# One of eight scalings of the scan's inputs made by GpSimd instead of ScalarE

## What is computed

```python
x = einsum('bld,ed->bel', ctx, in_proj_w)            # (4, 512, 512)
u = silu(causal_conv4(x) + conv_b)
dt_low, Bm, Cm = split(einsum('bdl,ed->bel', u, x_proj_w), [16, 32], axis=1)
dt = softplus(einsum('brl,dr->bdl', dt_low, dt_proj_w) + dt_proj_b)
A = -exp(A_log)                                      # (512, 16)
def step(state, inp):                                # over the 512 positions
    d, b, c, u = inp
    state = state * exp(d[..., None] * A) + (d * u)[..., None] * b[:, None, :]
    return state, einsum('bdn,bn->bd', state, c)
y = (ys + D * u) * silu(layernorm(x0))
```

## Time and profile before

| | us |
|---|---|
| median of 3 runs | 1756.34 |
| lowest, highest | 1755.08, 1762.23 |
| the profiled execution | 1761.8 |
| its span, from the first to the last instruction | 1759.7 |
| scan loop in the profile: first scan, last product | 59.5 to 505.9 |
| mean granted TensorE clock over the span | 0.927 of full |

### The profile page before, as it was taken

How to read it: one execution, slowest core, us unless ns; L and a number is a source line. 1 busy time by engine, 2 the same in 40 slices (tenths; PEclk the granted TensorE clock), 3 DMA queues, 4 the chain that set the end, 5 groups by cost and what they waited for, 6 DMA issues and landing times. The chain is left out here.

```text
span 1759.7 us, 22630 instructions
## 1 busy us (share of the span) xinstructions
PE 1540.0 (88%) x6580; PEld 669.6 (38%) x6581; DVE 1177.1 (67%) x1726; ACT 1006.3 (57%) x1551; POOL 518.1 (29%) x314
## 2 busy tenths in 40 slices
PE   5688878879857999999998789589999999898997
PEld 1334334334432444444443333123333333244543
DVE  7688988989885222222225749568888888369875
ACT  3798988979933001111113332357777777678775
POOL 1478678678860710000005446340000000000000
PEclk7698988979978999999999889689999999999999
DMA  5101102002472545458526453543332333020000
GB/s 176 42 31 46 51 19 67 18 13 72 137 255 94 191 62 190 150 177 274 177 85 200 130 126 112 199 79 79 74 84 71 83 74 81 29 96 1 31 30 36
DMA packets 105352, 173.47 MB, mean 99 GB/s; under 512 B 18323, under 2 KB 52499, under 8 KB 104259
## 3 DMA queue, kind: packets, MB, share of 16 engines
q1 hardware_dynamic: 83750, 124.62, 24.4%
q0 software_dynamic: 6624, 23.14, 4.4%
q10 hardware_dynamic: 14912, 24.89, 4.2%
HBM read 109.29 MB, written 54.92 MB: 93 GB/s over the span
## 5 line engine op out<-in xcount | busy, mean ns | idle before, releaser
L1582 DVE TENSOR_REDUCE a_mx<-a_s 128x2 f32<-128x1024 f32 x256 | 301.1, 1218 | 58.5 <-PE a_s L1704 57.0
L255 POOL TENSOR_TENSOR m_hs<-m_hs,m_C 128x1024 f32<-128x1024 f32 x128 | 301.3, 2367 | 117.0 <-DVE m_hs L447 116.4
L447 DVE TENSOR_TENSOR_SCAN m_hs<-m_dA,m_d 128x512 f32<-128x512 f32 x256 | 296.9, 1205 | 53.6 <-PE m_d L584 32.9
L859 ACT ACTIVATE e_sg<-e_gu 128x256 f32<-128x256 f32 x63 | 24.2, 383 | 312.8 <-PE e_gu L1091 312.8
L584 PE MATMUL m_d<-ident_sb,m_dBuT 128*128 128x128 f32 x1024 | 169.4, 300 | 27.4 <-ACT m_dBuT L332 14.4
L584 PEld LDWEIGHTS m_d<-ident_sb,m_dBuT 128*128 128x128 f32 x1024 | 122.4, 151 | 176.3 <-DVE m_hs L447 104.9
L1724 PE MATMUL a_t<-ring_sb 99*128 99x512 bf16 x512 | 181.1, 393 | 7.2 <-ACT early_sb L1486 3.8
L1486 ACT ACTIVATE a_pr<-a_t 128x512 f32<-128x512 f32 x256 | 142.3, 596 | 63.1 <-PE a_t L1724 61.9
L353 ACT ACTIVATE m_dA<-m_dt,m_negA 128x512 f32<-128x512 f32 x256 | 170.4, 712 | 7.7 <-DVE m_hs L447 7.6
L1704 PE MATMUL a_s<-ring_sb 96*128 96x512 bf16 x512 | 152.8, 390 | 24.3 <-DMA ring_sb<-qk_dram 14.1
L1486 ACT ACTIVATE early_sb<-a_t 128x512 f32<-128x512 f32 x256 | 142.2, 596 | 51.6 <-PE a_t L1724 50.6
(11 more groups left out here) (308 smaller groups left out, 2386.3 us busy)
## 6 DMA issues: line engine op xcount, KB each, us to landing
ring_sb<-qk_dram SPq DMA_DIRECT2D x384, 64.0 KB, 2.8
e_w<-in_ex_gu SPq DMA_DIRECT2D x16, 1024.0 KB, 6.7
xg_dram<-zeros_sb SPq DMA_DIRECT2D x2, 6016.0 KB, 28.5
e_xg<-xg_dram ACTq DMA_DIRECT2D x47, 256.0 KB, 2.7
yg_dram<-e_yo ACTq DMA_DIRECT2D x47, 256.0 KB, 2.0
m_C<-c_dram SPq DMA_DIRECT2D x64, 128.0 KB, 2.9
m_dt<-m_dt SPq DMA_DIRECT2D x64, 128.0 KB, 2.4
e_w<-in_ex_dn SPq DMA_DIRECT2D x16, 512.0 KB, 8.3
```

Source lines behind the costliest of these rows:

```text
L255: pool.tensor_tensor(hs[:, J % RH], hs[:, J % RH], C2[:, N % RC].unsqueeze(1).broadcast_to([P, 2, L]), ALU.mult).then_inc(s_hc, 1)
L447: dve.tensor_tensor_scan(hs[:, J % RH, h], dA[:, j % RA], pd[j % RD][:], 0.0, ALU.mult, ALU.add)\
L1582: dve.tensor_reduce(mx[:, r % 2, h * TB + 2 * c:h * TB + 2 * c + 2], psc[c][:], AX.X, ALU.max)\
```

## The change

GpSimd makes scaling 7 of every pair from 1 on, ScalarE keeps 0 to 6. In GpSimd's loop the scaling of pair N + 1 stands in the pair's second iteration (et = 1), ahead of the product of that iteration and after `add_relu` and `times_u`. It waits for the turned copies of its batch and for TensorE to have turned all inputs of the pair that used the slot of `dBuT` before. TensorE's first turn of a pair now waits for `s_sp` too, and so do ScalarE's copies over `BT` and `dtuT` two batches later. The whole diff:

```diff
--- before.py
+++ after.py
@@ -42,10 +42,13 @@
     RH, RA, RC, RD = 4, 8, 4, 3
     AHEAD = RA // 2 - 1
     R0, B0, C0, RX = 0, 32, 64, 96
-    ON_ACT = {0: (0, 1), 1: (2, 3), 2: (4, 5), 3: (6, 7)}
+    ON_ACT = {0: (0, 1), 1: (2, 3), 2: (4, 5), 3: (6,)}
 
     def by_act(N):
-        return 3 + 8 * N
+        return 3 + 7 * N
+
+    def by_pool(N):
+        return 2 + N
 
     with ExitStack() as ctx:
         def sb(name, shape, dt=F32):
@@ -249,6 +252,12 @@
                     add_relu(p, (s - 14) // 3)
                 if p < B and s in (15, 18, 21, 24):
                     times_u(p, (s - 15) // 3)
+                if et == 1 and N + 1 < B * PAIRS:
+                    pool.wait_ge(s_dttc, E4 * ((N + 1) // PAIRS + 1))
+                    pool.wait_ge(s_btc, (N + 1) // PAIRS + 1)
+                    if N >= 1:
+                        pool.wait_ge(s_dbu, 2 * E4 * N)
+                    scale_input(N + 1, 7)
                 if et == 0:
                     pool.wait_ge(s_c[N % RC], 32 * (N // RC + 1))
                 pool.wait_ge(s_scan, 2 * J + 2)
@@ -299,6 +308,7 @@
                 act.wait_ge(s_bt, p + 1)
                 if p >= 2:
                     act.wait_ge(s_sa, by_act(PAIRS * (p - 1) - 1))
+                    act.wait_ge(s_sp, by_pool(PAIRS * (p - 1) - 1))
                 src = (py[1] if p == 0 else pm)[:, 0:TB * RX].rearrange("p (t e) -> p t e", t=TB)
                 act.activation(BT[:, p % 2], src[:, :, B0:B0 + NS], ACT.Copy).then_inc(s_btc, 1)
 
@@ -575,9 +586,9 @@
                 j, g = 2 * J + h, 2 * et + h
                 if et == 0 and h == 0:
                     pe.wait_ge(s_sa, by_act(N))
+                    pe.wait_ge(s_sp, by_pool(N))
                     if N == 0:
                         pe.wait_ge(s_sv, 3)
-                        pe.wait_ge(s_sp, 2)
                 if j >= RD:
                     pe.wait_ge(s_scan, j - RD + 1)
                 for t in range(TB):
```

## The result

The changed kernel takes 1764.38 us (median of 12 runs, 1759.83 to 1767.86) against 1756.05 us (12 runs, 1753.66 to 1762.36). The ratio is 1.0043, 95% interval 1.0028 to 1.0057: 7.5 us slower, 5 to 10 (the medians lie 8.3 us apart). The forecast was 1759.4, 3.1 us slower. On two later occasions the same pair gave 1.0054 (1.0033 to 1.0075) and 1.0050 (1.0031 to 1.0068). The profiled execution, the longest of the 12, took 1767.86 us with a span of 1765.8, 6.1 us more than that of before. The scan loop in it ends 7.5 us later, at 513.4.

What follows compares the result with a forecast made beforehand. No engine a steady bound in batches 1 to 3 (VectorE sets the pace), ScalarE and GpSimd both full in the last; -1.8 + 4.9 = +3.1 us on the median of 1756.34 gives 1759.4, range 1753 to 1767.

Steps and rivals of the forecast that it cites:

- The price of GpSimd's scaling: Scan loop: each scaling adds 1.54 us to GpSimd, with 2.11 as upper and 0.80 as lower end.
- (a): Scan loop: GpSimd's scaling costs 0.80 us or less, sum -0.6 us, time 1752 to 1756; chance 0.12.
- (b): Scan loop: GpSimd's scaling takes 2.11 us, +6 to +8 us in all, time 1762 to 1764; chance 0.15.
- The last batch: From product 104 on GpSimd is full: 24 products and 5 scalings take 63.8 us, the end comes 4.9 us later.
- The boundaries: Pair boundary after the gates and SiLUs, once in each of batches 1 to 3: 0.4 us saved, together -1.3 us.
- The end of batch 1: Two ScalarE scalings fewer give at most 1.2 us, GpSimd's two extra operations take some back: -0.5 us.
- The rest of batches 1 to 3: GpSimd's added scalings there are hidden by its idle time or by the slack before the scan: 0 us.
- Batches 1 to 3 were to be shorter: Expected sign in the new profile: batches 1 to 3 each shorter by half a microsecond.
- longer batches 1 to 3: Listed sign that the prediction is wrong: batches 1 to 3 of the scan loop get longer; no size given.
- rival (c): Last batch: TensorE loses its clock while waiting for GpSimd's scalings, 10 us, time 1769; chance 0.15.

Runs made afterwards that it cites:

- experiments 2 and 4: 2: changed kernel with GpSimd's scaling for pairs 1 to 24 only or 25 to 31 only, 1.0042 each; 4: ScalarE keeps eight, GpSimd writes an unread tile, 1.0036.
- experiment 3: Kernel before, with scaling 7 left out for pairs 2 to 31 and none on GpSimd: 0.9996, in a repeat 0.9983.
- the copy: Changed kernel, but ScalarE makes all eight scalings and GpSimd makes its extra one into a tile nobody reads: 1.0036, in a repeat 1.0035.
- `gpsimd_first3`: Changed kernel, but GpSimd makes scaling 7 for pairs 1 to 24 only and ScalarE all eight for pairs 25 to 31: 1.0042.
- `gpsimd_even_pairs`: Changed kernel, but GpSimd makes scaling 7 for even pairs only and ScalarE for odd ones: 1.0033.

## Why the prediction was right, and what it had wrong

- **The price of GpSimd's scaling.** Taken as 1.54 us from the second of two rows. Measured 1.57 alone and 1.53 in a run. Rivals (a) and (b) are out. What the Trainium skill's page "GPSIMD Engine Reference", section 4.1, says of one-input operations, that they run roughly at line rate, holds for none of the 33: each takes at least twice the 0.77 us of its section 3.1.
- **The last batch.** Forecast 63.8 us from product 104, which starts 0.6 us earlier after the stall. Measured 63.76, and 0.61. This step was +4.9 and is +4.8 to +4.9, and experiments 2 and 4 show it to be GpSimd's time alone.
- **The boundaries.** Forecast 0.4 us in each of three. Measured 0.61 each (76.16 to 74.32). I had limited it to TensorE's idle time of 0.46 us, and that was too tight: its turns can start before the recorded end of the matmuls ahead. From the start of those matmuls (L537) to the turn were 2.34 us (210.78 to 213.12), now 1.73 (213.42 to 215.15), the whole 0.61 less. VectorE's 0.79 us of waiting at that place is 0.18 now:

```profile
215.90 1.22 DVE L458 TENSOR_TENSOR_SCAN m_hs<-m_dA,m_d 128x512 f32<-128x512 f32 x1 [0.18 <-ACT m_dA L364]
```

- **The end of batch 1.** Forecast -0.5. Slots 24 to 34 took 28.67, 29.28, 29.27 before and 28.86 to 28.88 after, -0.2. Without GpSimd's work (experiment 3) it is 27.5 to 28.0, so GpSimd gave most of the gain back there, as argued, a little more of it than counted.
- **The rest of batches 1 to 3: the term that failed.** I put GpSimd's side there at 0, and the copy shows nothing else: its series part is no longer than before. What the sum had no term for is that the series part could grow when ScalarE has less to do. With seven scalings on ScalarE it is longer in the mean, whoever makes the eighth: after the change 3.5 us in the mean of three profiles against three (168.4 and 164.9). Batches 1 to 3 were to be shorter by half a us each; the product of slot 100 came 2.7 and 2.6 us later in the first two pairs of profiles and 0.25 earlier in the third. By the prediction's own list, longer batches 1 to 3 were a sign of being wrong, and this one was met.

With these, the difference of the two kernels' mean loop is 4 x -0.61 + 5.5 + 3.5 and 0.1 for all other sections, +6.6 us, where the runs say 7.5 (5 to 10). The forecast of 1759.4 lies 5 us below the measured 1764.4: 3.5 of it are this one term, the rest isn't told from chance. The forecast difference of 3.1 us lies outside the measured interval, and the range reached up to +11 only for rival (c), whose 10 us didn't come: without that rival the upper end would have been (b)'s 1764, and that the time lies in the range is in part luck. Rival (c) had the right suspect in the wrong place (its 1.3 us a slot should also have been 3.9 less 2.34, 1.56). In the last batch the clock fell once (1.80 us sums, the granted clock 0.97), and the products behind it kept GpSimd's pace. In the series part a cycle at the low clock took 1.1 us more, and there the clock had been low for a part of the time before.

What stays open is why the clock should be low more often with one instruction less on ScalarE, and whether it always is: no run isolates it, and 13 profiles show the shift by its mean only. That `gpsimd_first3` measured +7.5 us and `gpsimd_even_pairs` +5.9 isn't explained either. Their loops were 2.5 and 0.8 us shorter than the mean of the kernel before, so 7 to 10 us are missing; both profiles are of executions 8 to 11 us faster than the median of their kernel.

## What to carry to other kernels

Before moving work from one engine to another, look for the stretch in which the receiver is full too: GpSimd was 72% busy in batch 2 and full where the other work thins out. Price such a stretch as count times pace of the receiver, from the last stall on; that sum held to 0.1 us here. And a gain on an engine that others seldom wait for is worth only the waits that end with it: 31 instructions of ScalarE, 14.9 us of its busy time, brought 2.4 us at the four places where others waited for it.

## What the runs showed of the hardware

- VectorE's 128x512 scalings and GpSimd's 128x1024 products slowed each other. A scaling that started 0.51 to 0.53 us before the end of a product took 0.80 to 0.81 us instead of 0.46, and the product that started beside a scaling 2.52 to 2.59 instead of 2.35 to 2.39. The Trainium skill's page "SBUF — State Buffer", section "SBUF: two separate sides", has the pair of ports they share locked for a whole instruction, so that the loser blocks. The 0.34 us lost here agree with that, since the product had 0.5 us left. The start of the stage doesn't: in the kernel before, VectorE's third scaling took 0.48 us (55.70 to 56.18) in the middle of GpSimd's scaling of 2.11 us (54.53 to 56.64).
- Pair boundaries and the last batch, at a granted clock of 0.90 to 1.00, repeated within 0.12 us from profile to profile and from chip to chip for the same code, one boundary of 28.4 instead of 26.8 us aside. The series part, where TensorE waits 2.5 us in every cycle and the granted clock is 0.74 to 0.86, took 163.2 to 166.0 us in seven profiles whose code is the same there up to an unread tile, and makes most of the loop's own scatter.
